# A joined graph network and mixer: paired tiles in the mix layers, a relu over four one-hots, fillers in the third edge pass

## The reference

```python
h = _layernorm(x, ln1_g[i], ln1_b[i])
q = softmax(split(h @ Wq[i]) * scale, axis=-1)   # over a head's 32 features
k = softmax(split(h @ Wk[i]) * scale, axis=-2)   # over the 3125 rows
v = split(h @ Wv[i])
context = einsum('bhnd,bhne->bhde', k, v)
x = x + einsum('bhnd,bhde->bhne', q, context) @ Wo[i] + bo[i]
h = _layernorm(x, ln2_g[i], ln2_b[i])
x = x + gelu(h @ W1[i] + b1[i]) @ W2[i] + b2[i]
```

## Time and profile before

| | |
|---|---|
| median of 3 runs | 4931.6 us (4924.03 to 4937.75) |
| profiled execution | 4926.91 us, its span 4925.1 us |
| mean granted TensorE clock | 0.866 |
| PE / PEld busy | 4107.5 us (83%) / 3374.2 us (69%) |
| DVE / ACT / POOL busy | 2728.7 us (55%) / 2479.2 us (50%) / 1587.4 us (32%) |

### The profile page before, as it was taken

One profiled execution on the slowest core, in us unless ns is written; L12 is line 12 of the kernel. 1 busy time (PEld: TensorE's weight loads), 2 busy tenths in 40 slices (PEclk: granted clock), 3 DMA queues, 4 the chain that ended last, 5 costly groups with the idle time before them and its releaser, 6 DMA issues. The chain is left out here.

```text
span 4925.1 us, 72874 instructions
## 1 busy us (share of the span) xinstructions
PE 4107.5 (83%) x20881; PEld 3374.2 (69%) x20882; DVE 2728.7 (55%) x8806; ACT 2479.2 (50%) x6813; POOL 1587.4 (32%) x1544
## 2 busy tenths in 40 slices
PE   9579999999998698988689998649936888888794
PEld 8568879879787477774467775349935666656793
DVE  2263272452632688884478886553354777767324
ACT  2343444534433699982489995213245555533222
POOL 0000000000000677760277772106517666610241
PEclk9789999999999899998899998659965666679797
DMA  5420000000001655541265554272266555522513
GB/s 145 126 86 11 19 10 1 19 10 1 19 6 30 162 152 150 144 120 39 78 155 146 147 151 103 61 227 70 62 150 170 148 146 145 146 57 64 181 36 90
DMA packets 260947, 465.88 MB, mean 95 GB/s; under 512 B 66637, under 2 KB 190471, under 8 KB 260110
## 3 DMA queue, kind: packets, MB, share of 16 engines
q1 hardware_dynamic: 172546, 258.16, 19.8%
q0 software_dynamic: 88064, 203.60, 16.1%
HBM read 400.72 MB, written 60.67 MB: 94 GB/s over the span
## 5 line engine op out<-in xcount | busy, mean ns | idle before, releaser
L667 POOL DMA_INDIRECT msg_rows<-tab_d,msg_cur x1296 | 1277.1, 985 | 1877.4 <-DVE msg_cur L143 1375.8
L943 PE MATMUL msg_agp<-msg_rows,msg_oh 125*125 125x261 f32 (+2 forms) x2592 | 819.3, 443 | 65.0 <-DVE ga_acc L819 52.5
L943 PEld LDWEIGHTS msg_agp<-msg_rows,msg_oh 125*125 125x125 f32 x2592 | 520.0, 213 | 201.3 <-DVE ga_acc L819 95.6
L896 PE MATMUL msg_zp<-g_xr,msg_oht 127*125 x1728 | 504.1, 395 | 91.7 <-ACT msg_oht L1013 69.5
L1004 ACT ACTIVATE msg_oh<-msg_dist,c_ones 125x125 f32<-125x125 f32 x1296 | 493.8, 387 | 0.0
L1000 ACT ACTIVATE msg_dist<-c_iota,c_rel 125x125 f32<-125x125 f32 x1296 | 493.6, 387 | 0.0
L896 PEld LDWEIGHTS msg_zp<-g_xr,msg_oht 127*125 127x125 f32 x1728 | 305.5, 189 | 147.2 <-issue 97.8
L819 DVE TENSOR_TENSOR gv_acc<-gv_acc,msg_agp 125x261 f32 (+1 forms) x864 | 359.9, 417 | 26.2 <-PE msg_agp L943 8.6
L1292 PE MATMUL mix_pb<-mix_ht,mix_w 128*128 128x125 f32 x3200 | 373.5, 275 | 0.0
L1301 PE MATMUL mix_pc<-mix_w,mix_ut 128*125 128x256 f32 x1600 | 361.8, 380 | 7.0 <-ACT mix_ut L1433 7.0
L1292 PEld LDWEIGHTS mix_pb<-mix_ht,mix_w 128*128 128x128 f32 x3200 | 365.7, 192 | 0.4
(11 more groups left out here) (556 smaller groups left out, 7550.7 us busy)
## 6 DMA issues: line engine op xcount, KB each, us to landing
msg_oht<-rel_d SPq DMA_DIRECT2D x81, 875.0 KB
msg_rows<-tab_d,msg_cur POOLq DMA_INDIRECT x1296
pl_raw<-in_edge_attr SPq DMA_DIRECT2D x25, 448.0 KB
msg_pens<-pen_d SPq DMA_DIRECT2D x270, 31.2 KB
msg_oht<-rel_d SPq DMA_DIRECT2D x81, 101.6 KB
mix_w<-in_L_mix_W SPq DMA_DIRECT2D x8, 1024.0 KB
m0w_wr<-in_L_ffn_w SPq DMA_DIRECT2D x16, 512.0 KB
m0w_w2r<-in_L_ffn_w SPq DMA_DIRECT2D x16, 512.0 KB
```

The lines of the kernel that those rows point to most:

```text
L667: nc.gpsimd.indirect_dma_start(out=rows_all[:, q, k, :], out_offset=None, in_=table, in_offset=bass.IndirectOffsetOnAxis(ap=cur[:, q, k:k ...
L896: last = nc.tensor.matmul(z, hots, d_t, start=True, stop=by_vector(k // 2))
L943: nc.tensor.matmul(agp[:, sum_bank(u, k), 0:AW], oh[:, u % RB, k, :], rows[:, u % RB, k, 0:AW], start=True, stop=True).then_inc(summed.sem, 1)
```

## The change

It has four parts, and the first three lie in `messages`.

1. `edge_hots` makes eight Abs before the first Relu, and each Relu covers four steps (125 x 500). The ring holds eight distances; `dist_used` guards it.
2. In pass 3 the scores of a group use one PSUM bank in place of three in turn, so scoring group j+1 waits until the logits of group j are read.
3. Pass 3 has a new matmul behind each `aggregate`: the identity times 256 columns of `iota`, into a bank that nothing reads.
4. `mix_layers` works on pairs of tiles (NP = 13, the last pair has one tile), with operands of 250 and 512 columns. PE no longer multiplies by Wv for each tile: `context` sums k times the normalised rows themselves, and the learned scale and shift, Wv and Wo are then applied to the 256 x 256 result. Queries are projected beside the context instead of ahead of it. The first two pairs of the next layer are normalised and turned before the last tile of this one is finished.

```diff
-        dist = st.sb("dist", [P, 4, P])
+        dist = st.sb("dist", [P, 8, P])
...
-                            pe.wait_ge(z_used.sem, z_used.at(g - 2))
-                        last = nc.tensor.matmul(zp[:, u % 3, k * heads:(k + 1) * heads], hots, d_t, start=True, stop=True)
+                            pe.wait_ge(z_used.sem, z_used.at(g))
+                        last = nc.tensor.matmul(zp[:, 0, k * heads:(k + 1) * heads], hots, d_t, start=True, stop=True)
...
                     nc.tensor.matmul(agp[:, sum_bank(u, k), 0:AW], oh[:, u % RB, k, :], rows[:, u % RB, k, 0:AW], start=True, stop=True).then_inc(summed.sem, 1)
+                    if not one:
+
+                        nc.tensor.matmul(zp[:, 1, 0:D], c.ident[0:P, 0:P], c.iota[0:P, 0:D], start=True, stop=True)
...
-                    for k in range(G + 1):
-                        if k < G:
-                            nc.scalar.activation(dist[:, k % 4, :], c.iota[0:P, 0:P], ACT.Abs, scale=-1.0, bias=c.rel[:, bass.ds(g * G + k, 1)]).then_inc(dist_ready.sem, 1)
...
-                        last = nc.scalar.activation(oh[:, u % RB, k - 1, :], dist[:, (k - 1) % 4, :], ACT.Relu, scale=-1.0, bias=c.ones[0:P, 0:1])
-                    last.then_inc(oh_ready.sem, 1)
+                    for b in range(5):
+                        if b >= 2:
+                            act.wait_ge(dist_used.sem, dist_used.at(g * 3 + b - 1))
...
+                        if b < 4:
+                            for k in range(b * QS, (b + 1) * QS):
+                                last = nc.scalar.activation(dist[:, k % 8, :], c.iota[0:P, 0:P], ACT.Abs, scale=-1.0, bias=c.rel[:, bass.ds(g * G + k, 1)])
+                            last.then_inc(dist_ready.sem, 1)
...
+                        last = nc.scalar.activation(oh[:, u % RB, (b - 1) * QS:b * QS, :], dist[:, (b - 1) % 2 * QS:((b - 1) % 2 + 1) * QS, :], ACT.Relu, scale=-1.0, bias=c.ones[0:P, 0:1])
+                        last.then_inc((dist_used if b < 4 else oh_ready).sem, 1)
...
-                    def project_tile(t):
...
-                        for w, (bank, lo) in enumerate(((2 * (t % 2), 0), (2 * (t % 2) + 1, 0), (2 * (t % 2) + 1, D))):
-                            for kc in range(2):
-                                last = nc.tensor.matmul(pb[bank][0:P, lo:lo + D], ht[:, t % HR, kc, :], wp[:, w, kc, :], start=(kc == 0), stop=(kc == 1))
...
+                    def keys(p):
+                        wait_half(pe, l, 0, p)
+                        if p >= 2:
+                            pe.wait_ge(k_taken.sem, at(k_taken, l, p - 1))
                         apart(pe, order)
+                        for t in tiles(p):
+                            for kc in range(2):
+                                last = nc.tensor.matmul(pb[p % 2][0:P, (t % 2) * D:(t % 2 + 1) * D], qts[:, kc, t * P:(t + 1) * P], wp[:, 1, kc, :], start=(kc == 0), stop=(kc == 1))
...
+                    for p in range(NP):
+                        if 2 <= p + 2 < NP:
+                            turn(l, 0, p + 2)
+                        keys(p)
+                    queries(0)
...
+                    for p in range(NP):
+                        if p + 2 < NP:
+                            queries(p + 2)
+                        context(p)
+                        if 1 <= p < NP - 1:
+                            turn_q(p - 1)
...
+                        for i in range(2):
+                            last = nc.tensor.matmul(pb[3][:, j * 128:(j + 1) * 128], wp[:, 2, i, j * 128:(j + 1) * 128], hct[:, i, j * 128:(j + 1) * 128], start=(i == 0), stop=(i == 1))
...
+                        if p == NP - 1 and l + 1 < LAYERS:
+                            for near in range(2):
+                                turn(l + 1, 0, near)
+                        for t in tiles(p):
+                            down_tile(t)
...
+                    for p in range(NP + 1):
+                        if p < NP:
+                            shift_q(p)
+                        if p == 1:
+                            dve.wait_ge(kmax_spread.sem, at(kmax_spread, l, 1))
+                            shift_k(0)
+                        if 1 <= p < NP:
+                            shift_k(p)
+                        if p >= 1:
+                            weigh_q(p - 1)
```

More of the change, by code:

```diff
@@ L1127, in mix_layers @@
         off = st.sb("off", [P, 2, NT])
-        pa = [st.ps(f"pa{j}", [128, 2, P]) for j in range(2)]
+        pa = [st.ps(f"pa{j}", [128, 512]) for j in range(2)]
         pb = [st.ps(f"pb{j}", [128, 512]) for j in range(4)]
@@ new lines, in keys, with queries @@
+                        last.then_inc(k_done.sem, 1)
+                    def queries(p):
+                        if p >= 2:
+                            pe.wait_ge(q_shifted.sem, at(q_shifted, l, p - 1))
+                            apart(pe, order)
+                        for t in tiles(p):
+                            for kc in range(2):
+                                last = nc.tensor.matmul(pb[2 + p % 2][0:P, (t % 2) * D:(t % 2 + 1) * D], qts[:, kc, t * P:(t + 1) * P], wp[:, 0, kc, :], start=(kc == 0), stop=(kc == 1))
+                        last.then_inc(q_done.sem, 1)
@@ L1273, in context @@
+                    def context(p):
+                        pe.wait_ge(k_exp.sem, at(k_exp, l, p + 1))
+                        for t in tiles(p):
+                            for j in range(2):
+                                last = nc.tensor.matmul(pb[j][:, 0:D + 1], kv[:, t, j * 128:(j + 1) * 128], kv[:, t, D:2 * D + 1], start=(t == 0), stop=(t == NT - 1))
+                        if p == NP - 1:
                             last.then_inc(ctx_done.sem, 1)
@@ L1366, in root @@
                         nc.scalar.activation(rstd[:, i, lo:hi], rstd[:, i, lo:hi], ACT.Sqrt).then_inc(std_ready.sem, 1)
-                    def turn_out(i, t):
-                        if t % 2 == 1:
-                            return
-                        act.wait_ge(turned.sem, at(turned, l, i * NT + t + 1))
-                        for j in range(2):
-                            last = nc.scalar.activation(ht[:, t % HR, j, :], pa[0][:, j, :], ACT.Identity, scale=gb[:, i, 0, j:j + 1], bias=gb[:, i, 1, j:j + 1])
-                        last.then_inc(half_a.sem, 1)
@@ new lines, in exp_k @@
+                    def exp_k(p):
+                        act.wait_ge(k_shifted.sem, at(k_shifted, l, p + 1))
+                        nc.scalar.activation(kv[:, rows_of(p), 0:D], kv[:, rows_of(p), 0:D], ACT.Exp, scale=scale).then_inc(k_exp.sem, 1)
+                    for p in range(NP):
+                        for t in tiles(p + 4) if p + 4 < NP else ():
+                            normalise(l, 0, t)
+                        if p + 2 < NP:
+                            turn_out(l, 0, p + 2)
+                        take_k(p)
@@ new lines, in turn_out @@
+                def turn_out(l, i, p):
+                    if p % 2 == 0:
+                        return
+                    dve.wait_ge(turned.sem, at(turned, l, i * NP + p + 1))
+                    n = size(p) * P
+                    for j in range(2):
+                        to = (qts[:, j, cols(p)], ht[:, p % 2, j, 0:n])[i]
+                        last = nc.vector.tensor_scalar(to, pa[1][:, j * n:(j + 1) * n], gb[:, i, 0, j:j + 1], gb[:, i, 1, j:j + 1], ALU.mult, ALU.add)
+                    last.then_inc(half_v.sem, 1)
```

478 lines of the change are left out of this document (232 added, 246 removed).

## The result

The changed kernel took 4726.8 us in the median of 4 runs (4713.5 to 4741.4) against 4934.4 for the kernel before on the same chip: a ratio of 0.9583, 95% interval 0.9549 to 0.9618. The forecast was 4720, in a range of 4675 to 4790.

What follows compares the result with a forecast made beforehand. It took PE to bound the mixer, a PE and DVE loop passes 1 and 2, and PE at low clock pass 3; -120 + 10 - 16 - 12 - 75 = -213 us gave 4720 us, range 4675 to 4790.

Steps and rivals of the forecast that it cites:

- Mixer, projection to context: Four mixer layers, first projection to end of context: 80 us a layer, 320 in place of 440.2, -120 us.
- Hand-over: Mixer stage after the context: added turns, wider ACT and DVE steps, passes and a mask, +2.5 us a layer, +10.
- Feed-forward: Mixer up and down stage: 32 passes of 250 columns for 64 of 125 a pair, -16 us taken.
- Between layers: Mixer, down to next projection: two prepared pairs leave only a DVE chain of about 1.7 us open, -12 us.
- Edge one-hots: Edge passes: ACT loses at least 3.3 us a group, hidden under PE's and DVE's loop, 0 us of time.
- the shares' rival: Passes 1 and 2: R3, ranking engines by busy share; ACT relieved by 3.3 us a group, kernel 4655 us, chance 0.06.
- Pass 3: Third edge pass: fillers raise PE's clock, POOL nearly full, period 24.08 to 21.2 us over 26 groups, -75 us.
- Everything else: Stretches the change doesn't touch, such as before the mixer and between passes: no term in the sum, 0 us.
- R1: Pass 3: clock stays at 1.2 GHz despite fillers, each group 14 us more, kernel about 5160 us, chance 0.04.
- R2: Pass 3: fillers give the clock and take the time back, period near 24 us, kernel 4794 us, chance 0.08.
- R3: Passes 1 and 2: ACT was the limit, period could fall from 21.6 to 20.3 us, kernel 4655 us, chance 0.06.
- R4: Mixer context: DVE takes 4.6 us a pair and stalls PE, 35 us more, kernel 4755 us, chance 0.12.

## Why the prediction was right, and where its terms were off

The forecast was -213 us, and the medians give -207.5. The mechanisms came as told: PE's work in the mixer, the clock and POOL in pass 3, no gain from ACT. That the total came within 7 us is in part luck, as two misses cancel: the mixer gave 18 us more than forecast (12 more by the average of all executions), and pass 3 gave 15 less.

**Mixer, projection to context: forecast -120, measured -130.** Four layers take 77.4 to 77.8 us, 310.1 in all, against 440.2. Keys took 27.1 where I took 28.5, and behind the maximum of k almost nothing of the 2.5 us was left: the queries of two pairs bridge it.

**Hand-over: forecast +10, measured +14.** In the kernel before the four hand-overs take 17.5 us, of which the prediction read a short one, 4.1. Now they take 31.6: 7.0 in layers 0 and 1, 8.9 and 8.7 in layers 2 and 3. In those two and the first tiles behind them the granted clock fell; windows of layer 2's and layer 1's hand-over:

```profile
932.40:941.30 8.90, 5.39 (x23) 3.85 (x21) 2.33 (x6) 3.16 (x5) 0.00 (x0) 0.67 0.00 0
646.70:653.70 7.00, 3.50 (x23) 2.50 (x21) 2.33 (x6) 3.16 (x5) 0.00 (x0) 1.00 0.01 2
```

The count of DVE and ACT work is the same; PE alone is slower. The prediction priced the longer chain at the high level throughout. Which layers fall differs by execution: in the run with half fillers, with the same mixer, only layer 3 does.

**Feed-forward: forecast -16, measured -26.** From the end of the last use to the end of the last down it takes 176.8 us in layer 1 (677.8 to 854.6), against 182.9 before (742.6 to 925.5). The other layers take 176.5, 176.7 and 175.5, and 182.9 each before. Why it is more than the 0.37 us a pair of the prediction was not looked into.

**Between layers: forecast -12, measured -15.** PE in the changed kernel:

```profile
851.05 3.62 PE L1338 MATMUL mix_pc<-mix_w,mix_ut 128*125 128x256 f32 x16
854.51 0.59 PE L1264 MATMUL mix_pa<-c_ident,mx_kv 125*128 125x125 f32 x4
854.94 1.89 PE L1276 MATMUL mix_pb<-mix_wp,mix_qts 128*125 128x256 f32 x8
```

No gap is left here, and 0.2 to 0.7 us from down to keys in all three places; 5.5 us stood there. I had left DVE's chain of 1.7 us open, but two prepared pairs cover it. With the uses at -1 these make -158, and 2 us come back between the last layer and pass 1. A layer's period is 286 to 290 us, forecast 292.

**Edge one-hots: forecast 0, measured 0.** The Relu's price was right, and the sum for ACT was not:

```profile
L1010 ACT ACTIVATE msg_dist<-c_iota,c_rel 125x125 f32<-125x125 f32 x1296 | 400.8, 388 | 5.3
L1015 ACT ACTIVATE msg_oh<-msg_dist,c_ones 125x500 f32<-125x500 f32 x324 | 227.1, 701 | 2.6
```

The Relu takes 701 ns, 0.70 forecast. But 32 activations of 0.387 never cost 12.2 us a group. Timeline of ACT in the kernel before, pass 1:

```profile
1910.62 0.39 ACT L1004 ACTIVATE msg_oh<-msg_dist,c_ones 125x125 f32<-125x125 f32 x1
1910.91 0.39 ACT L1000 ACTIVATE msg_dist<-c_iota,c_rel 125x125 f32<-125x125 f32 x1
1911.20 0.39 ACT L1004 ACTIVATE msg_oh<-msg_dist,c_ones 125x125 f32<-125x125 f32 x1
```

One starts 0.29 us behind the other, before its end, so 32 took about 9.3, and a group saves (274.36 - 247.84) / 14 = 1.9. ACT's waits in 300 us of pass 1 of the changed kernel:

```profile
ACT msg_ex L994 <- DVE msg_delta L794: 49.7, 14, 3.9
```

The wait for `delta` grew by as much, from 24.7. The wait that the prediction read was the better witness than the shares, and even the shares' rival would have had only half its relief.

**Pass 3: forecast -75, measured -60.** The mechanism was right: fillers, clock at 1.00, POOL in front and PE close behind. The period was 21.8 and not 21.2, by two steps of the sum. First, POOL's gather was taken at 1.018 us from the kernel before, where POOL still waited for sums. There 68 of 274 gathers meet a scale, and none starts less than 0.39 us behind it. In 400 us of the changed kernel 10 start 0.04 to 0.10 us behind it and take 1.97 to 2.03 us each; the mean is 1.044, so 21.6. Second, the sum sets the mean of all 26 periods, 24.08, against a floor of the steady ones, and counts the gain 26 times. The first two periods took 26.5 and 28.8 before and take 27.1 and 27.5 now, so they gave 0.7 us in place of 5.8. PE's 19.1 was a little low too: it is busy for 475.5 of 500 us, or 20.4 in a steady period of 21.4.

**Everything else: forecast 0, measured +28 in the profiled pair.** 7 lie ahead of the mixer, a stretch that took from 270.4 to 283.2 us in the profiles with the new mixer. 18 lie between pass 1 and pass 2, on the clock. Three windows of 20 us before, then at the same place after:

```profile
2245.00:2265.00 20.00, 19.95 (x44) 10.90 (x45) 3.17 (x16) 0.21 (x1) 0.00 (x0) 0.52 0.87 185
2265.00:2285.00 20.00, 15.90 (x46) 8.57 (x44) 5.91 (x26) 2.77 (x7) 0.00 (x0) 0.73 0.00 0
2285.00:2305.00 20.00, 19.72 (x59) 11.57 (x59) 6.45 (x29) 2.77 (x7) 0.00 (x0) 0.76 0.00 1
```

```profile
2097.00:2117.00 20.00, 17.91 (x38) 9.91 (x39) 2.74 (x14) 0.21 (x1) 0.00 (x0) 0.50 1.00 211
2117.00:2137.00 20.00, 16.41 (x35) 8.35 (x34) 5.47 (x24) 2.77 (x7) 0.00 (x0) 0.50 0.00 0
2137.00:2157.00 20.00, 20.00 (x43) 11.20 (x43) 5.47 (x24) 2.77 (x7) 0.00 (x0) 0.50 0.00 0
```

The stretch took 246 us in the execution of before and 250 with the new mixer alone, but 264.0, 263.6 and 264.0 with the one-hots, the bank or the fillers alone, and 260 to 265 in the variants of the changed kernel. It falls on kernels with either mixer and either pass 3, so I take it for a difference of executions. But in the ten profiles from the other chips the two short ones are just the two kernels whose `messages` is that of before, and all eight with any part of the change in it are long, so a cause in the code is not excluded. Against it speaks the chip on which everything took longer: there the kernel with fillers of 192 columns has a clock of 0.74 from 40 to 80 us behind the last exponential of pass 1, as before, and its sister with 256 columns 0.50, though the two differ only in pass 3, which comes later. It was not repeated with one kernel, and that is argued, not shown.

**The rivals.** R1 (the fillers hurt) and R2 (pass 3 gains nothing) fall with the fillers alone. R3 (ACT was the limit) falls with the one-hots alone. R4 (DVE stalls the context) did not occur, but its mechanism is real: 3.8 us a layer away.

## What to carry to other kernels

A matmul that waits for nothing can be worth its time where PE waits for others and runs at the low clock. Here 16 x 0.43 us of them in each group bought 60 us in the pass. Fillers of half or three quarters the width brought the clock down again and gained nothing, and twice as many cost 6 us a group: raise what they cost only up to the engine that limits next. Sum an engine's work from its start-to-start times, since the mean of a group counts overlapping instructions twice. When a floor is worked out from a steady stretch, hold it against the steady period and not against the mean of the pass. A cover by another engine holds to its last microsecond, so name how much of it is left.

## What the runs showed of the hardware

A gather on POOL takes 0.95 us alone. When it starts 0.04 to 0.97 us behind a DVE `tensor_tensor` of 1.25 us with both operands in SBUF, it takes from 1.11 to 2.03 and ends 2.06 to 2.08 behind that one's start. With one operand in PSUM it takes 0.94 to 0.95. Half the rows make it 0.91 alone: its time is hardly in the rows.

Two ACT activations of 125 columns that don't depend on each other start 0.29 us apart, each 0.39 long.

One chip ran all kernels 10% slower, with single instructions as long as elsewhere (the scale 1.25 us, a gather 0.95) and gaps of up to 5 us at `issue`. The kernels with the new mixer and the fillers stayed faster than the one before there, with a smaller gain (a ratio of 0.969 to 0.975, against 0.958 for the changed kernel on the first). Its cause is open.
